# Two weight fetches of one kernel, taken apart: the MLP's first weights are fetched back earlier, and each layer waits for its own

## The reference, cut to what matters

```
h = gelu(layer_norm(x) @ mlp_w1.T + mlp_b1);  x + h @ mlp_w2.T + mlp_b2      # mlp_w1 1024x256, mlp_w2 256x1024
top1 = argmax(x.mean(axis=1) @ Wr + br)                                       # one expert of 8 per sequence
h = relu(x @ W1[top1] + b1[top1]);  out = h @ W2[top1] + b2[top1]             # W1 256x1024, W2 1024x256
```

## Time and profile before

| | |
|---|---|
| median of three runs | 3584.11 us |
| the profiled execution | 3576.54 us, its span 3574.4 us |
| PE, POOL busy | 3014.5 us (84%), 2789.7 us (78%) |
| DVE, ACT busy | 2631.6 us (74%), 2416.0 us (68%) |
| TensorE clock granted, mean | 0.916 of full |
| DMA | 736.59 MB, mean 206 GB/s |
| fetches back of `w_1` and `w_2` after an expert | 12 of each |

### The profile page before, as it was taken

One profiled execution on the slowest core, in us unless ns is written; L12 is line 12 of the kernel. 1 busy time (PEld: TensorE's weight loads), 2 busy tenths in 40 slices (PEclk: granted clock), 3 DMA queues, 4 the chain that ended last, 5 costly groups with the idle time before them and its releaser, 6 DMA issues.

```text
span 3574.4 us, 58031 instructions
## 1 busy us (share of the span) xinstructions
PE 3014.5 (84%) x17392; PEld 1884.2 (53%) x17392; DVE 2631.6 (74%) x5920; ACT 2416.0 (68%) x5331; POOL 2789.7 (78%) x2583
## 2 busy tenths in 40 slices
PE   5789888888989988898898889888898998987557
PEld 3555454554655556465565546555464654654236
DVE  3356879787787868778787877878687787878870
ACT  5577778676767767776785777777687776864431
POOL 1118989888888888888898888888898888977880
PEclk9898899899999999999899899989999999998779
DMA  2017878778877787877787788777878778888981
GB/s 74 7 55 204 231 196 226 205 206 254 212 218 206 214 234 210 253 201 207 225 232 231 192 254 214 213 221 201 254 207 253 207 195 226 222 264 246 296 240 37
DMA packets 423337, 736.59 MB, mean 206 GB/s; under 512 B 53427, under 2 KB 100147, under 8 KB 423027
## 3 DMA queue, kind: packets, MB, share of 16 engines
q1 hardware_dynamic: 423026, 732.89, 73.6%
HBM read 648.84 MB, written 83.89 MB: 205 GB/s over the span
## 4 chain that ended last, share of the span: by engine, by line
PE 61%; DVE 10%; issue 8%; ACT 7%; DMA 6%; POOL 6%; SPq 2%; DVEq 0%; ACTq 0%; POOLq 0%
PE bank L482 18%; PE bank L490 9%; PE bank L752 6%; PE bank L605 6%; PE bank L738 5%; PE bank L515 4%; PE bank L686 4%; PE bank L527 4%; DMA w<-in_mlp_w2T 3%; DVE u_rows L1303 3%; POOL u_rows L1522 3%; PE bank L543 2%; ACT prob L807 2%; POOL u_rows L1515 2%; DMA u_rows<-u_dram 2%
## 5 line engine op out<-in xcount | busy, mean ns | idle before, releaser
L1522 POOL TENSOR_TENSOR u_rows<-u_rows,c_rows 128x512 f32<-128x512 f32 x1024 | 1303.7, 1276 | 196.4 <-DVE state L1308 128.7
L1515 POOL TENSOR_TENSOR u_rows<-u_rows,b_rows 128x512 f32<-128x512 f32 x960 | 1224.6, 1277 | 142.0 <-DMA u_rows<-u_dram 132.8
L978 ACT ACTIVATE bank<-d_rows,a_rep 128x512 f32<-128x512 f32 x1024 | 695.3, 687 | 310.8 <-DMA d_rows<-delta_dram 135.0
L1303 DVE TENSOR_TENSOR_SCAN u_rows<-bank,state,u_rows 128x512 f32<-128x512 f32 x512 | 641.7, 1270 | 66.3 <-ACT bank L978 54.6
L1303 DVE TENSOR_TENSOR_SCAN u_rows<-bank,u_rows 128x512 f32<-128x512 f32 x512 | 621.8, 1214 | 72.8 <-ACT bank L978 63.6
L807 ACT ACTIVATE prob<-prob,neg_max 128x256 f32<-128x256 f32 x1024 | 509.6, 504 | 25.0 <-DVE neg_max L1090 25.0
L1090 DVE CUSTOM_DVE_ANT_0 prob<-bank,band 128x256 f32<-128x256 f32 x896 | 335.8, 416 | 114.3 <-PE bank L515 71.9
L527 PE MATMUL bank<-ident,prob 128*128 128x128 f32 x2048 | 326.2, 289 | 109.5 <-ACT prob L807 80.0
L527 PEld LDWEIGHTS bank<-ident,prob 128*128 128x128 f32 x2048 | 240.1, 146 | 279.3 <-issue 228.1
L686 PE MATMUL bank<-u_rows,sum_n 128*32 128x512 f32 x2048 | 291.4, 643 | 83.7 <-POOL u_rows L1522 75.7
L515 PE MATMUL bank<-kT,q_own 32*128 32x256 f32 x2048 | 297.0, 409 | 22.0 <-DVE yg L1317 9.0
(11 more groups left out here) (167 smaller groups left out, 5071.3 us busy)
## 6 DMA issues: line engine op xcount, KB each, us to landing
u_rows<-u_dram SPq DMA_DIRECT2D x1024, 256.0 KB, 5.5
d_rows<-delta_dram SPq DMA_DIRECT2D x1024, 256.0 KB, 5.7
w<-in_W SPq DMA_DIRECT2D x28, 1024.0 KB, 7.9
zs_dram<-region_b SPq DMA_DIRECT2D x64, 256.0 KB, 4.5
xc_dram<-region_b SPq DMA_DIRECT2D x64, 256.0 KB, 3.6
u_dram<-region_b SPq DMA_DIRECT2D x64, 256.0 KB, 5.4
delta_dram<-region_b SPq DMA_DIRECT2D x64, 256.0 KB, 5.6
yg<-xc_dram SPq DMA_DIRECT2D x64, 256.0 KB, 4.1
```

Source lines behind the costliest of these rows:

```text
L978: e.activation(banks[at.bank][:, :], delta_of(i, k), ACT.Exp, scale=a_rep[:, j:j + 1]).then_inc(filled[at.bank], 1)
L1303: e.tensor_tensor_scan(rows, banks[at.bank][:, :], rows, state[:, k:k + 1] if i % 2 else 0.0, ALU.mult, ALU.add).then_inc(drained[at.bank], 1)
L1515: e.tensor_tensor(rows, rows, b_rows[:, :], ALU.mult).then_inc(bx_ready.sem, 1)
L1522: e.tensor_tensor(rows, rows, c_rows[:, :], ALU.mult).then_inc(hc_ready.sem, 1)
```

## The change

The fetch of the MLP's `w_1` moves from step 24 of the expert to step 20 of SP's walk, behind a wait that PE has finished e1.3. The fetch of `w_2` stays in step 24, behind the output store. The one semaphore `w_back` becomes two; PE waits for `mlp_w1_back` ahead of h0 and, new, for `mlp_w2_back` ahead of m0.

```diff
-        w_back = sem("w_back", 2, 16)
+        w1_back = sem("mlp_w1_back", 1, 16)
+        w2_back = sem("mlp_w2_back", 1, 16)
...
             if i >= 4:
-                e.wait_ge(*w_back.at(i - 4, 2))
+                e.wait_ge(*w1_back.at(i - 4, 1))
             for m in range(KF):
...
             e.wait_ge(*hidden.at(i, 2))
+            if i >= 4:
+                e.wait_ge(*w2_back.at(i - 4, 1))
             for t in range(GT):
...
         def sp_expert(e, i):
             for half in range(2):
-                yield from range(12)
+                yield from range(8)
+                if half and i + 4 < 2 * BATCH:
+                    e.wait_ge(*full(uses["expert", i, "e1.3"]))
+                    e.dma_start(*MLP_WEIGHTS[0]).then_inc(w1_back.sem, 16)
+                yield from range(4)
...
                 if half and i + 4 < 2 * BATCH:
-                    for dst, src in MLP_WEIGHTS:
-                        e.dma_start(dst, src).then_inc(w_back.sem, 16)
+                    e.dma_start(*MLP_WEIGHTS[1]).then_inc(w2_back.sem, 16)
             yield
```

## The result

| | before | after |
|---|---|---|
| median of the runs shown together, us | 3582.68 (3579.66 to 3599.53, 8 runs) | 3563.97 (3557.23 to 3569.91, 8 runs) |
| ratio, 95% interval | | 0.9947 [0.9927, 0.9967] |
| profiled execution, us | 3576.5 | 3561.02 |
| its span, us | 3574.4 | 3558.8 |

The change takes 18.7 us off; 3565 had been forecast. Three sections of the page answer to the earlier trace rows: busy us by engine; the chain that ended last, by line; the fetches with KB each and median us to landing. Lines have moved down by one to six (482 is 483, 686 is 689, 978 is 981, 1060 is 1063, 1515 is 1518).

What follows compares the result with a forecast made beforehand. No engine is full; at the transitions the queue of transfers was taken as the bound. 21.2 us of wait less 2.4 for the clock gives 18.8, about 19: 3584.1 - 19 = 3565 us, range 3549 to 3580.

Steps and rivals of the forecast that it cites:

- The wait ahead of h0: PE's 12 waits for the MLP's weights, 34.5 us in all, each fall to 1.11 us: 21.2 us less.
- `w_1` is there, the w_2 wait is free: `w_1`, issued 22 us earlier, lands before h0 needs it; the new `w_2` wait ahead of m0 costs nothing.
- The queue's price, 4.1 us per MB: Each 1 MB fetch delays transfers behind it by 4.1 us; removing one from the old place gives that back to later loads.
- Both waits of ACT and POOL go: At the transition, waits for the last scan tile, 2.87 us (ACT) and 2.91 (POOL), vanish as loads get up to 4.6 earlier.
- The store is not last behind h0: Delta store that ACT's bias copy needs lands near 1285.2, before h0 ends at 1288.4; otherwise up to 1.3 us lost per transition.
- Tile 57 in time: The `d_rows` load behind the moved fetch lands after 10.5 us, before ACT's use, with 0.6 us to spare.
- rival 3: Tile 57 comes late behind the moved fetch, delaying ACT, DVE's scan and the norm; 3594 us if 2.4 late; chance 0.06.
- The clock gives back 2.4 us: Earlier h0 and following sums run at PE's low clock in the 12 transitions, 0.2 us lost each, 2.4 in all.
- The sum lasts to the end: The 18.8 us gained at the transitions carries over in full to the kernel's end, through PE's own products.
- Rival 2: The next transition, paced by POOL, gives PE's gain back as a longer wait: 3577 to 3584 us; chance 0.14.
- Rival 1: DVE's line 1060, held by POOL's port lock, changes its long passages: 3551 or 3579 us; chance 0.15 better, 0.12 worse.

Runs made afterwards that it cites:

- the kernel with one more MB: Changed kernel plus an unused 1 MB HBM-to-HBM copy ahead of the moved fetch: 3562.69 us, 0.9949; with accumulating norms too, 3505.14 us, 0.9787.
- the split alone: Kernel before plus only the two semaphores and separate waits, both fetches at the old place: 3572.64 us, 0.9977; with accumulating norms too, 3501.82 us, 0.9786.
- the moved fetch left out: Changed kernel without fetching `w_1` back, so MLPs from group 4 on multiply with the expert's leftover weights: 3568.31 us, 0.9957.
- the two kernels with the edited norms: Kernels before and after, with DVE's two small operations of each layer norm also writing an accumulator: 3538.54 us (0.9878) and 3501.63 us (0.9787).
- the swapped order: Two semaphores, both fetches at the old place, accumulating norms, but `w_2` issued ahead of `w_1`: 3542.02 us, 0.9892.

## Why the prediction was right, step by step

The mechanism held: the wait went, down to ACT's copies, and the time followed. That the median was met to 1 us (3563.97 for 3565) is luck beside it: the interval of the ratio leaves room for a gain of 12 to 26 us, and what was wrong about the queue, below, happened to have no effect that can be told.

- **The wait ahead of h0, 21.2 us.** Right: 21.1 in the traces. Taking the idle time of the MLPs without a fetch as the floor gave it, where the whole wait (34.5) or its share of the chain (3% of 3574, 107 us) would have been far too high.
- **`w_1` is there, the w_2 wait is free.** Right: the fetches are 21.84 us apart and neither wait shows up.
- **The queue's price, 4.1 us per MB.** About right in the new place, for the load it was meant for: tile 57's landed 3.8 us later (9.6 for 5.8), the two behind it less; a second MB added 0.3 to it, and the slowest load took 1.7 more. Too high in the old place: with `w_1` gone, `w_2` takes 8.4 us for 10.4, so 2.0 less. Why less comes back there was not tested. The figure of 6.15 us in the Trainium skill, "DMA: Bandwidth & Descriptors", section Bandwidth, which stands there for transfers issued from GpSimd, would have made tile 57 late; the trace does not agree, tile 57 is used without a wait even behind 2 MB.
- **Both waits of ACT and POOL go.** Wrong in size: 2.87 became 1.16 and 2.91 became 1.41. For ACT the 1.71 us come from an issue that is 0.67 earlier beside the transposes (4.38 us ahead of them for 3.71) and a landing 1.04 faster (8.53 us after the issue, 1273.22 to 1281.75, for 9.56), where I had counted 0.5 and 4.1. It had no consequence that can be told: waits of this kind cost nothing in the kernel with one more MB.
- **The store is not last behind h0.** Wrong in size, right in effect. In the transition shown it takes 6.3 us for 7.8, so 1.5 less and not 4.6, and lands near 1284.4, with the end of h0 (1284.37) and not 3 us ahead of it. Three of the 12 bias copies are released by it, as many as before, and in the split alone all 12, without cost. (By the prediction's own times the loss to be feared was 1289.8 - 1288.4 = 1.4 us, not 1.3.) In the transition shown the copy ends at 1285.34, while PE is at the sums of 1284.30 (to 1285.37).
- **Tile 57 in time, rival 3.** Right, with the margin understated: 1.6 us where 0.6 was counted, mostly because its load had taken 5.8 us before and not the 6.4 of the slowest. One more MB left 0.4. The queue is full in the gap of the earlier trace rows, so that is where the loads pushed back are caught up.
- **The clock gives back 2.4 us.** Neither shown nor refuted. The earlier h0 runs as slowly as the later one did (3.68 for 3.75 in the transition shown). Over the 12 transitions h0 took 43.7 us for 44.1 and the sums behind it 16.7 for 15.9, and h0 to the end of m3 grew by 0.6. But between kernels whose h0 starts equally early this last figure goes from 685.7 (the kernel after) to 691.2 (the moved fetch left out), so single traces can't tell 0.6 from 2.4. Sums near 1.5, which the prediction took for most of the 12, were half of them; the others took 1.06 us already.
- **The sum lasts to the end.** Right, and shown: 35.9 us of idle sum against 36.9 measured (the two kernels with the edited norms), and 29.0 against 38 to 40 for the swapped order, of which 9 us are unexplained. Rival 2, the gain given back, would have made those far smaller.
- **Rival 1, line 1060.** It did not turn this comparison, but it is real: it is the likeliest reason why the split alone looked like half the change, and without its long form the same change is worth 37 us instead of 19. (Its place is 113 us behind h0, 1399.55 - 1286.15, and not 60.) That the stall is what scatters and costs was shown by taking it away: the accumulating form never takes longer than 0.159 us in that kernel's b norms. That it is the port is argued: the Trainium skill, "SBUF — State Buffer", section SBUF: two separate sides, has DVE's two-port forms and POOL lock each other out, and the trace agrees, since every long one ends with POOL's first gap (last section). That the edit works through the lock and not through something else in the form was not tried.

Why 19 and 37 are different is worth a sentence. In these traces the end of the weights' transfer goes with SP's place in its list and with the queue, the arrival of PE at h0 with the norms. Part of what the faster norms gain turns into a longer wait for the weights (34.5 to 49.3 us) as long as h0 waits for both. So the two edits bring 80 us together, and 43 and 19 alone.

## What to carry to other kernels

A semaphore that counts two transfers makes the first user wait for the last byte of both: give each transfer its own, and issue them in the order of first use. Here the split gave the whole gain, an earlier fetch nearly as much, and the order alone was worth 38 to 40 us. To price a wait, look for the same instruction in a passage where the releaser is absent: the difference of the idle times is the gain, and not the wait, nor the share in the chain. When two versions differ by less than a recurring random stall costs, remove the stall in both, and then compare.

## What the runs showed of the hardware

A `tensor_scalar` of 4 elements a row on DVE took up to 7.11 us beside a busy POOL, and 0.156 to 0.159 us at all 32 places of the b norms when it also wrote an accumulator, plus 0.083 us for reading that out. The profile of before shows how the long one ends (timelines of DVE and POOL, start us, us): it lasts until POOL, which goes from one instruction to the next, comes to a gap.

```profile
1399.55 4.97 DVE L1060 TENSOR_SCALAR rstd_b<-mean_var_b 128x4 f32<-128x4 f32 x1
```

```profile
1398.47 2.35 POOL L1554 TENSOR_TENSOR x<-x,e_b 128x1024 f32<-128x1024 f32 x1
1400.79 1.26 POOL L1515 TENSOR_TENSOR u_rows<-u_rows,b_rows 128x512 f32<-128x512 f32 x1
1402.02 1.25 POOL L1522 TENSOR_TENSOR u_rows<-u_rows,c_rows 128x512 f32<-128x512 f32 x1
1403.24 1.25 POOL L1515 TENSOR_TENSOR u_rows<-u_rows,b_rows 128x512 f32<-128x512 f32 x1
1405.86 1.27 POOL L1522 TENSOR_TENSOR u_rows<-u_rows,c_rows 128x512 f32<-128x512 f32 x1 [1.36 <-DVE u_rows L1303]
```

DVE's ends at 1404.52, and POOL's gap is from 1404.49 to 1405.86. The four instructions of POOL from 1398.47 on follow each other without a gap, and the short one of DVE, in progress from 1399.55, did not get in between them. It is so at all 11 places of this profile and all ten of the kernel after: no gap of POOL lies within the long one, over four to six POOL instructions, and it ends 0.02 to 0.03 us behind the start of the first gap. (Long means over 2 us.)

And a transfer of 1 MB put ahead of loads of 256 KB made the first `d_rows` load behind it take 9.6 us for 5.8, while a second MB made that 9.9: the second one cost this load far less than the first, and less than the 4.1 us that lay between two such transfers' own landings.
